# Wide feature products, w6 folded into w8, and the last labels shared by two engines in an attentive recommendation kernel

## What is computed

```python
def _attn_pool(x, mask, w_a, b_a, w_b):
    score = jnp.exp((x @ w_a + b_a) @ w_b)
    score = jnp.where(mask == 0, PAD, score)
    p = jax.nn.softmax(score, axis=1)
    return jnp.einsum('bne,bn->be', x, p[..., 0])
q1 = _attn_pool(x, mask, w1, b1, w2)
q2 = _attn_pool(x, mask, w3, b3, w4)
h = jnp.concatenate([q1, q2], axis=1) @ w5 + b5
f6 = h @ w6 + b6
cross = h[:, iu] * h[:, ju] * g          # all 44,850 pairs i < j
f7 = cross @ w7 + b7
out8 = jnp.concatenate([f6, f7], axis=1) @ w8 + b8
return jnp.einsum('bu,bku->bk', out8, label_embedding)
```

## Time and profile before

| | us |
|---|---|
| median of 3 runs | 1992.28 |
| lowest, highest | 1981.65, 1993.16 |
| profiled execution | 1983.79 |
| its span | 1982.0 |

### The profile page before, as it was taken

One profiled execution on the slowest core, in us unless ns is written; L12 is line 12 of the kernel. 1 busy time (PEld: TensorE's weight loads), 2 busy tenths in 40 slices (PEclk: granted clock), 3 DMA queues, 4 the chain that ended last, 5 costly groups with the idle time before them and its releaser, 6 DMA issues.

```text
span 1982.0 us, 25089 instructions
## 1 busy us (share of the span) xinstructions
PE 1685.8 (85%) x7476; PEld 1230.0 (62%) x7476; DVE 1458.6 (74%) x5702; ACT 881.6 (44%) x2513; POOL 41.4 (2%) x86
## 2 busy tenths in 40 slices
PE   1446999999999999999999999999899999996000
PEld 0324677777777677777776777777677777773000
DVE  8755998889972257778753677787447777875998
ACT  5335776676854344444433444444244443541000
POOL 0001000100100100000000000000000000000000
PEclk9667999998999999999998999999999999998555
DMA  6426666565744789999996799999868999996993
GB/s 262 174 90 246 228 232 255 211 269 236 285 181 156 272 341 358 358 372 372 409 330 224 284 363 365 359 391 408 271 243 328 359 363 356 420 387 219 395 393 157
DMA packets 112005, 590.73 MB, mean 298 GB/s; under 512 B 13940, under 2 KB 29069, under 8 KB 81661
## 3 DMA queue, kind: packets, MB, share of 16 engines
q1 hardware_dynamic: 81373, 368.22, 49.8%
q10 hardware_dynamic: 27680, 217.89, 28.4%
q0 software_dynamic: 2816, 3.01, 0.4%
HBM read 585.28 MB, written 3.79 MB: 297 GB/s over the span
## 4 chain that ended last, share of the span: by engine, by line
PE 78%; DVE 14%; DMA 4%; issue 2%; ACT 1%; SPq 1%; POOL 0%; ACTq 0%; DVEq 0%; POOLq 0%
PE bank L525 68%; DVE stream L845 8%; PE bank L496 5%; DVE junk L753 4%; DMA sring<-hrows 3%; PE bank L481 2%; PE bank L507 1%; DVE cring L825 1%; PE bank L538 1%; DMA wring<-in_w7p 1%; PE bank L469 1%; ACT absjunk L603 0%; POOL hrows L442 0%; SPq L369 0%; DMA hrows<-hT 0%
## 5 line engine op out<-in xcount | busy, mean ns | idle before, releaser
L525 PE MATMUL bank<-wring,cring 128*128 128x300 f32 x5616 | 1459.2, 422 | 34.0 <-DVE cring L825 26.8
L525 PEld LDWEIGHTS bank<-wring,cring 128*128 128x128 f32 x5616 | 1078.6, 193 | 403.1 <-DVE cring L825 33.4
L669 ACT ACTIVATE wring<-wring,gcol 128x300 f32<-128x300 f32 x1404 | 635.8, 532 | 779.6 <-DMA wring<-in_w7p 419.1
L845 DVE SCALAR_TENSOR_TENSOR stream<-stream,out 128x300 f32<-128x300 f32 x1600 | 644.2, 465 | 3.9 <-ACT out L590 3.9
L825 DVE TENSOR_TENSOR cring<-lefts,sring 128x1024 f32<-128x1024 f32 (+2 forms) x232 | 274.7, 1187 | 177.6 <-PE bank L525 165.1
L753 DVE SCALAR_TENSOR_TENSOR junk<-stream,ubc 128x300 bf16<-128x300 f32 x896 | 357.1, 466 | 0.0
L825 DVE TENSOR_TENSOR cring<-hT,sring 128x1024 f32<-128x1024 f32 (+1 forms) x120 | 144.5, 1206 | 175.4 <-PE bank L525 141.6
L603 ACT ACTIVATE absjunk<-stream 128x300 bf16<-128x300 f32 x448 | 195.7, 439 | 3.4 <-issue 2.2
L845 DVE DVE_READ_ACCUMULATOR stream<-stream,out 128x1 f32 x1600 | 130.8, 82 | 0.0
L481 PE MATMUL bank<-stream,wts 128*32 128x300 f32 x896 | 66.9, 454 | 63.2 <-DVE small L795 63.2
L496 PE MATMUL bank<-poolT,w5sb 128*128 128x64 f32 (+3 forms) x576 | 95.9, 306 | 3.1 <-ACT poolT L590 3.1
(11 more groups left out here) (51 smaller groups left out, 225.1 us busy)
## 6 DMA issues: line engine op xcount, KB each, us to landing
stream<-in_label SPq DMA_DIRECT2D x320, 750.0 KB, 6.9
wring<-in_w7p ACTq DMA_DIRECT2D x164, 1200.0 KB, 8.5
stream<-in_x SPq DMA_DIRECT2D x64, 1050.0 KB, 9.2
sring<-hrows SPq DMA_DIRECT2D x76, 512.0 KB
wring<-in_w7p ACTq DMA_DIRECT2D x8, 1050.0 KB, 6.7
wring<-in_w7p ACTq DMA_DIRECT2D x8, 600.0 KB, 6.8
sring<-hrows SPq DMA_DIRECT2D x16, 176.0 KB
lefts<-hrows SPq DMA_DIRECT2D x20, 128.0 KB, 5.8
```

What stands on the lines that cost most here:

```text
L525: mm = pe.matmul(acc[(g * GB + b) % 4][:, 0:E], lhs, w, start=(t == 0), stop=(t == NT - 1))
L669: ins = nc.scalar.activation(w, w, ACT.Copy, scale=gcol[:, t:t + 1])
L845: ins = nc.vector.scalar_tensor_tensor(out=row_in, in0=row_in, scalar=1.0, in1=out8[:, m % (2 * GB), :], op0=ALU.mult, op1=ALU.mult, accum ...
```

## The change

1. **Wide w5 products.** `poolT` holds four halves. In phase 0 the w5 product and the features of a group are made once, after its fourth half, with 256 columns (36 records as before). The head stays at one half at a time. Each output chunk now has a bank and an eviction of its own, and ScalarE's two stores go out after the first chunk. In phase 0 MIX_OUT comes at the step of MIX (12), before at 14; TURN_OUT at 10 instead of 11.
2. **w6 folded.** In the head, at step 9 behind the pooling of half 0, TensorE computes w6 times the upper part of w8, and b8 + b6 times it (`fold_w8`); ScalarE evicts them (`folded_out`). out8 is then begun from the features themselves. `linear`, `linear_out` and `f6T` go. w6 is handed over transposed.
3. **Head steps apart:** new distances, and four more steps at the end of the head.
4. **A third slot** in `sring`.
5. **Tail.** From chunk 240 on, four of every five chunks are multiplied by VectorE in one instruction (5 x 300), and ScalarE sums each of the five rows with a copy that has an accumulator output (`sums`). The fifth chunk stays with VectorE alone, the last one too.

```diff
-    SSLOTS = 2
+    SSLOTS = 3
-        f6T = sb("f6T", [P, NCH, L])
-        poolT = sb("poolT", [P, 2, NCH, 2, P // 2])
+        poolT = sb("poolT", [P, NCH, 2, L])
+        FIRST_SHARED = (NBT - GB) * LC
+        SHARED = [n >= FIRST_SHARED and n % 5 != 4 and n < NBT * LC - 1 for n in range(NBT * LC)]
-            return {-1: x_end(-1, GS - 1) + 8, G: TAIL_STEPS}.get(ph, NU)
-
-        EXP, SOFT, MAX, WEIGH = (0, 0), (1, 1), (1, 1), (2, 2)
-        POOL, DEN, POOL_OUT = (2, 3), (6, 8), (6, 8)
-        TURN, TURN_OUT = (6, 9), (6, 11)
-        MIX, MIX_OUT = (6, 12), (6, 14)
-        X_LOAD = (3, 4)
+            return {-1: x_end(-1, GS - 1) + 12, G: TAIL_STEPS + OUT8_OUT + 1}.get(ph, NU)
+
+        EXP, SOFT, MAX, WEIGH = (0, 0), (3, 1), (2, 1), (3, 2)
+        POOL, DEN, POOL_OUT = (3, 3), (6, 8), (7, 8)
+        TURN, TURN_OUT = (7, 9), (8, 10)
+        MIX, MIX_OUT = (8, 12), (8, 12)
+        X_LOAD = (4, 4)
+        W68 = 9
...
+            def mix(s0, n_half):
+
+                b0, nb = s0 % GS * (P // 2), n_half * (P // 2)
+                pe.wait_ge(side_ev, ops[0])
+                for o, n in CHUNKS:
+                    dst = side_bank()
                     for q in range(2 * NCH):
                         nk = CHUNKS[q % NCH][1]
-                        mm = pe.matmul(dst[0:n, c * P // 2:(c + 1) * P // 2], w5sb[0:nk, q, o:o + n],
-                                       poolT[0:nk, s % 2, q % NCH, q // NCH, :],
+                        mm = pe.matmul(dst[0:n, 0:nb], w5sb[0:nk, q, o:o + n],
+                                       poolT[0:nk, q % NCH, q // NCH, b0:b0 + nb],
                                        start=(q == 0), stop=(q == 2 * NCH - 1))
-                mm.then_inc(side_mm, 1)
+                    mm.then_inc(side_mm, 1)
+
+            def fold_w8():
+
+                pe.wait_ge(w_in, 16 * 12)
                 for o, n in CHUNKS:
                     dst = side_bank()
                     for c, (_, nk) in enumerate(CHUNKS):
-                        mm = pe.matmul(dst[0:n, 0:L], w6sb[0:nk, c, o:o + n], hT[0:nk, g, c, :],
+                        mm = pe.matmul(dst[0:n, 0:E], w6T[0:nk, c, o:o + n], w8sb[0:nk, c, :],
                                        start=(c == 0), stop=(c == NCH - 1))
                     mm.then_inc(side_mm, 1)
+                dst = side_bank()
+                pe.matmul(dst[0:1, 0:E], ones[:, 0:1], b8row[:], start=True, stop=False)
+                for c, (_, nk) in enumerate(CHUNKS):
+                    mm = pe.matmul(dst[0:1, 0:E], bcol[0:nk, 1, c:c + 1], w8sb[0:nk, c, :],
+                                   start=False, stop=(c == NCH - 1))
+                mm.then_inc(side_mm, 1)
...
-                    pe.matmul(dst[:, 0:E], f6T[0:n, c, b * P:(b + 1) * P], w8sb[0:n, c, :], start=False, stop=False)
+                    pe.matmul(dst[:, 0:E], hT[0:n, g, c, b * P:(b + 1) * P], w68[0:n, c, :], start=False, stop=False)
...
                     for s in after_half(ph, u, *MIX):
-                        mix(s)
+                        if ph == -1:
+                            mix(s, 1)
+                        elif s % GS == GS - 1:
+                            mix(s - GS + 1, GS)
...
+            def features_out(s0, n_half):
+                g, b0, nb = s0 // GS, s0 % GS * (P // 2), n_half * (P // 2)
                 for c, (_, n) in enumerate(CHUNKS):
                     src = side_bank()
-                    biased(f6T[0:n, c, :], src[0:n, 0:L], bcol[0:n, 1, c:c + 1]).then_inc(side_ev, 1)
+                    biased(hT[0:n, g, c, b0:b0 + nb], src[0:n, 0:nb], bcol[0:n, 0, c:c + 1]).then_inc(side_ev, 1)
+                    if c == 0 and s0 % GS + n_half == GS:
+                        act.wait_ge(side_ev, ops[0])
+                        act.dma_start(hrows[g][A0:A0 + P], hT[:, g, 0, :]).then_inc(a_stored[g], 16)
+                        act.dma_start(hrows[g][A0 + P:A0 + A_ROWS], hT[0:A_ROWS - P, g, 0, :]).then_inc(a_stored[g], 16)
+                act.wait_ge(side_ev, ops[0])
+                act.sem_inc(h_ready, n_half)
...
+            def sums(n):
+
+                m, q0 = n // LC, n % LC * LR
+                act.wait_ge(l_product, released(n)[1])
+                for k in range(LR):
+                    row = lring[:, n % LSLOTS, k, :]
+                    ins = nc.scalar.activation(row, row, ACT.Copy, accum_out=score[:, m % GB, q0 + k:q0 + k + 1])
+                ins.then_inc(l_summed, 1)
...
+                    if ph == G and u > OUT8_OUT:
+                        n = FIRST_SHARED + u - OUT8_OUT - 1
+                        if SHARED[n]:
+                            sums(n)
...
+                if SHARED[n]:
+                    if r == 0:
+                        rows = lring[:, n % LSLOTS]
+                        nc.vector.tensor_tensor(rows, rows, out8[:, m % (2 * GB), :].unsqueeze(1).to_broadcast([P, LR, E]),
+                                                ALU.mult).then_inc(l_product, 1)
+                    return
```

More of the change, by code:

```diff
@@ L104, with rec_kernel @@
 UNIT_TILE = [sum(u[3] for u in UNITS[:k]) for k in range(NU + 1)]
-def rec_kernel(nc, x, label, w13, w24, w5, w6, w8, bcols, b8, w7p, vleft, vright, out):
+def rec_kernel(nc, x, label, w13, w24, w5, w6t, w8, bcols, b8, w7p, vleft, vright, out):
     B, N, _ = x.shape
@@ L176, in rec_kernel @@
         w5sb = sb("w5sb", [P, 2 * NCH, E])
-        w6sb = sb("w6sb", [P, NCH, E])
+        w68 = sb("w68", [P, NCH, E])
         w8sb = sb("w8sb", [P, 2 * NCH, E])
@@ L186, in rec_kernel @@
         ones = sb("ones", [1, P])
+        b8row = sb("b8row", [1, E])
         brow = sb("brow", [1, E])
@@ L201, in rec_kernel @@
         vl, vr, vp = (scratch[:, k * NT * VC:(k + 1) * NT * VC] for k in range(3))
+        w6T = scratch[:, 3 * NT * VC:3 * NT * VC + NCH * E].rearrange("p (c e) -> p c e", e=E)
         A_ROWS, B_ROWS = P + 64, P + 96
@@ L249, in rec_kernel @@
         l_used = sem("l_used")
+        l_product = sem("l_product")
+        l_summed = sem("l_summed")
         out_stored = [sem(f"out_stored{k}") for k in range(2)]
@@ L285, in labels_by, with released @@
             return GB * K * max(0, u + 1 - LABEL_FROM) // (NU - LABEL_FROM)
+        FIRST_SHARED = (NBT - GB) * LC
+        SHARED = [n >= FIRST_SHARED and n % 5 != 4 and n < NBT * LC - 1 for n in range(NBT * LC)]
+        def released(n):
+            return (l_summed if SHARED[n] else l_used), sum(SHARED[k] == SHARED[n] for k in range(n + 1))
         def x_end(ph, s):
@@ L408, in _ @@
                         if n + LSLOTS < NBT * LC:
-                            sp.wait_ge(l_used, n + 1)
+                            sp.wait_ge(*released(n))
                             l_load(n + LSLOTS)
@@ L444, in scores_out @@
             def scores_out(m):
-                pool.wait_ge(l_used, (m + 1) * LC)
+                ends = [max(n for n in range((m + 1) * LC) if SHARED[n] == kind) for kind in set(SHARED[:(m + 1) * LC])]
+                for n in ends:
+                    pool.wait_ge(*released(n))
                 pool.dma_start(out_v[m], score[:, m % GB, :]).then_inc(out_stored[m % GB], 16)
@@ L556, in _ @@
                         pool_rows(s)
+                    if ph == -1 and u == W68:
+                        fold_w8()
                     for s in after_half(ph, u, *TURN):
@@ L569, in _ @@
                             out8_from_f7((ph - 1) * GB + b)
-                    if 0 <= ph < G and u == F6:
-                        linear(ph)
                     if 0 <= ph < G and u == OUT8_START:
                         pe.wait_ge(pool_out, NS)
-                        pe.wait_ge(side_ev, ops[0])
+                        pe.wait_ge(h_ready, GS * (ph + 1))
                         if ph >= 1:
@@ L623, in pools_turned @@
             def pools_turned(s):
[L624 removed]
+                src, b = side_bank(), s % GS * (P // 2)
                 for c, (_, n) in enumerate(CHUNKS):
[L626 removed]
+                    ins = cp(poolT[0:n, c, :, b:b + P // 2].rearrange("p h (j u) -> p h j u", u=UB),
                              src[0:n, c * P:(c + 1) * P].rearrange("p (j h u) -> p h j u", h=2, u=UB))
                 ins.then_inc(side_ev, 1)
[L630 to L640 removed]
@@ L647, in f7_turned, with folded_out @@
+            def folded_out():
+                for c, (_, n) in enumerate(CHUNKS):
+                    src = side_bank()
+                    cp(w68[0:n, c, :], src[0:n, 0:E]).then_inc(side_ev, 1)
+                src = side_bank()
+                cp(brow[:], src[0:1, 0:E]).then_inc(side_ev, 1)
             def f7_turned(b):
@@ L696, in _ @@
                         pools_out(s)
+                    if ph == -1 and u == W68:
+                        folded_out()
                     for s in after_half(ph, u, *TURN_OUT):
@@ L700, in _ @@
                         act.wait_ge(w_in, 16 * 12)
-                        features_out(s)
+                        if ph == -1:
+                            features_out(s, 1)
```

(8 more changed lines are left out.)

25 lines of the change are left out of this document (4 added, 21 removed).

## The result

The changed kernel takes 1915.93 us (median of 4 runs, 1911.56 to 1916.95), the one before 1992.72 (median of 4). The ratio is 0.9616, 95% interval 0.9588 to 0.9644: 77 us or 3.8% faster. The forecast was 1903, in a range of 1883 to 1937.

What follows compares the result with a forecast made beforehand. Bounds: TensorE and VectorE together in phase 0, TensorE in phases 1 to 3, VectorE in the tail. Gains 0.5 + 11.2 + 18.8 + 38.7 + 15.2 = 84.4 us, 1983.8 to 1899.4 profiled; median forecast 1903, range 1883 to 1937.

Steps and rivals of the forecast that it cites:

- The head: Start to features complete: new waits for ScalarE eat what moved steps give; end at 156.8 instead of 157.3, gain 0.5 us.
- TensorE to VectorE in phase 0: Phase 0 until unit 75's product: VectorE takes over as the bound; gain 11.2 us (bounds 0 and 18.8).
- the new wait at units 36 and 61: Phase 0: exponentials stand behind ScalarE's wait for the wide product, costing VectorE 3.8 us, twice 7.6.
- The rest of phase 0: After unit 75's product: 84 us instead of 102.8, TensorE no longer three units in arrears; gain 18.8 (15 to 22).
- The rule on hidden weight loads: w5 products: skill says next weights load under the running matmul, so wide saves nothing; prediction took the trace, 33 us saved.
- Three slots: Ends of phases 1 to 3: earlier row loads remove stops and slow records; with the w6 saving, gains 38.7 us.
- unit 89 some 18 after it: Phase ends with three slots: unit 89's product some 18 us after unit 87's, while TensorE still has work.
- rival C: Memory sets phases 1 to 3; boundary gains of 24.6 us vanish: 1924 us; chance 0.08.
- The tail: After the phases: ScalarE sums 320 rows and is the later engine at 141.4 us; gain 15.2 us.
- rivals D: Tail: ScalarE's sums are slow, 0.532 us each, 30 us above the forecast tail: 1929 us; chance 0.10.
- F: Tail: a row's activation and accumulator read do not overlap on f32, 0.72 us a row, slower kernel: 1990 us; chance 0.04.
- span-based sum: Whole kernel: stage gains add to 84.4 us, taking the profiled execution from 1983.8 to 1899.4 us.

Runs made afterwards that it cites:

- later-features run: Changed kernel with the features of phase 0 evicted one step later (step 13 instead of 12): 1912.51 us, 0.959 to the kernel before.
- thinned labels: Changed kernel with label chunks asked for from step 84 on in phases 1 to 3 loaded with one row of five, result partly wrong: span 1907.3 us, one execution.
- narrow run: Changed kernel with phase 0's w5 product and features made half by half (64 columns, twelve times) instead of once a group: 1950.0 us, 0.9764.
- run 48: Not a run number: 48 counts unit records in the narrow run, the changed kernel with phase 0's w5 product and features made half by half: 1950.0 us, 0.9764.
- four-slot run: Changed kernel with four row slots instead of three: 1913.8 us, 0.9618 to the kernel before.
- run with the three edits: Changed kernel with fold at step 10 of phase 0, head features at step 11 and phase 0 features at step 13: 1894.83 us, 0.9507.

## Why the prediction was right, and where it was off

**The head: right, in most of its steps too.** The poolings of halves 1, 2 and 3 start at 86.33, 116.50 and 142.46 us, worked out were 85.2, 115.6 and 141.9; the fold ran from 53.79 to 61.7, forecast 53.5 to 60. Waits worked out as 1.6, 10.4 and 4.8 us measure 3.35, 10.01 and 4.44. A fourth wait, 9.04 us before the weights of half 3, was not in my working. The two experiments that take either cause away (fold out of the head: 9 us; features behind the second exponential: 16 us) show that these are the causes of the head having won nothing.

**TensorE to VectorE in phase 0: right in kind, 6.5 us off.** The bound changed hands: VectorE's busy time is 342.7 us (before 343.2), and TensorE shows 28.1 us of waits for its products, 20 of them (waits of TensorE, 207 to 560 us):

```profile
PE bank L546 <- DVE cring L867: 28.1, 20, 3.6
```

The step that was mis-sized is the new wait at units 36 and 61: 3.8 us each, measured 6.75 and 8.46. I had put TensorE right behind VectorE, one unit late, and left out the pooling of 3.7 us that comes two steps earlier and was in my own list of its work. With it the wide product ends 17.9 us after unit 36's start (352.75 to 370.6), not 14.7. The later-features run takes 12.2 us of waits away and brings unit 75 forward by 11.3.

**The rest of phase 0: right**, 84.7 for 84.

**The rule on hidden weight loads.** The Trainium skill ("TensorE: Matmul & The Clock Gate", "Step-by-step: what each phase is for") would have the wide form save nothing. The wide product took 9.66 us (forecast 9.4) for four of 4.78 or more. The measurement decides: in float32 a 64-column product does not come at the price of its columns.

**Three slots: right in direction, 9.9 us too good.** The step that was mis-sized is "unit 89 some 18 after it", counted from unit 87. Measured are 26.6 and 26.7 us. I had taken the 12.7 us of one older request for those of unit 89; from the end of unit 88's product to unit 89's 14.8 us pass in phase 1 and 19.7 in phase 2. In phase 1 unit 88 was late as well, 10.6 us after unit 87 for 5.7. The miss is all in this term: without the slot the other edits brought 12.6 us to these phases for 14.1, the slot 15.7 for 24.6. The thinned labels show that the missing part is DMA shared with labels: with them out of the way the phases take 364.8, and my 364.4 stands as the floor. So rival C, in the form that I gave it (memory sets the phases), is wrong, and a smaller form of it is true: DMA was busy 0.93 there, and that showed in the latency of the small row loads, not in the rate of the phase.

**The tail: right.** 64 products of 1,500 elements and the sums, as groups of the tail: busy us, mean ns.

```profile
L704 ACT ACTIVATE stream<-stream 128x300 f32<-128x300 f32 x320 | 139.4, 449 | 0.0
L889 DVE TENSOR_TENSOR stream<-stream,out 128x1500 f32<-128x1500 f32 x64 | 105.8, 1712 | 4.9 <-ACT out L614 4.9
L704 ACT ACTIVATION_READ_ACCUMULATOR stream<-stream 128x1 f32 x320 | 63.7, 199 | 0.0
```

and two sums in a row:

```profile
1766.07 0.45 ACT L704 ACTIVATE stream<-stream 128x300 f32<-128x300 f32 x1
1766.42 0.19 ACT L704 ACTIVATION_READ_ACCUMULATOR stream<-stream 128x1 f32 x1
1766.51 0.44 ACT L704 ACTIVATE stream<-stream 128x300 f32<-128x300 f32 x1
```

They start 0.44 us apart, as the magnitudes do; rivals D (0.53) and F (0.72) are out. The figure of 0.55 us that the prediction quotes beside D (the Trainium skill, "ScalarE: Activation LUTs", "Rules for kernel authors") is stated for a bias read from a pointer operand. The sums have none, and the length of one is 0.449 us; only the w7 scaling, with its scale read so, comes near it with 0.532. ScalarE is the later engine: 1766.07 to 1905.6, 139.5 us for 139.7 worked out.

**Offset.** I put the forecast of the median 4 us above the span-based sum, because the median of before was 8.5 above its profiled execution. The sum was 17.6 us too low in span: 66.8 us of gain for 84.4, with every stage's error on the same side. By medians the gain is 76.8 us. That the forecast of 1903 is off by 13 us only comes from those 4 us, which no stage gave, and from two profiled executions that lie differently to their medians; it is luck, and not better working.

## What to carry to other kernels

When two engines are at their limit together, relieving one is worth only the distance to the other, plus the arrears it no longer carries into the next stage; that second part was the larger here. An eviction placed in the product's own step blocks its engine for the whole product: look at what stands behind it in that engine's order, and put the short urgent instruction first (one number, 14 us in the head). A load with slack in a nearly full DMA still lands late; here neither asking for it sooner (the fourth slot) nor holding back the early ones shortened the program beyond the error when it was done alone, but holding them back shortened the two phases in which it was done by 2.4 us each.

## What the runs showed of the hardware

**The clock after narrow products.** With products of 64 columns the granted clock of phase 0 is 0.95 and 0.91 (twelve narrow ones) against 0.99 and 1.00 (three wide ones), although TensorE is busier in the first case. In the narrow run 48 unit records behind one narrow set take 13.91 us, and behind others between 12.3 and 15.0, against 12.12 at the full 2.4 GHz. If the narrow sets are the reason, part of a wide product's value is that the stretch behind it is not slowed. That narrow columns are the reason, and not the sum of ScalarE's waits, is argued from the place of the drops, not isolated.

**A clock drop without a stop.** In the four-slot run the clock was at 0.70 in ten busy us at the end of phase 2 (9.75 of 10 us busy), where out8 is begun: six of its records took 3.46 us instead of 1.98 straight behind busy time. In the run with the three edits six such records took 3.66 us at the end of phase 0, again with no stop before them. What lowered the clock stays open.

**Small loads in a full DMA.** From unit 88's product, behind which the last rows of unit 89 are asked for, to unit 89's, 16.0 us pass in phase 1 (1001.02 to 1017.03) and 20.9 in phase 2 (1365.35 to 1386.29), with thinned labels 10.9 (1358.75 to 1369.69). The label loads themselves land after 9.8 us in the middle of the new tail, at 417 GB/s, and after 6.0 in the old one, at 394.
